# Row additions of a mixture-of-experts phase: two DMAs of 512 columns against four of 256, and loads that wait for a landing

## The chip, the cores and the metric

One core of a Trainium2 chip runs the whole program. The metric is the device time of one execution in microseconds (us), lower is better. The kernel before takes 1786.95 us, the median of 3 runs (1781.33 to 1793.82).

## What is computed

The input has 16 x 256 = 4096 rows of 512 floats. Four residual layers follow each other: a cross-attention over latents, a LoRA layer with gates, an attention with 8 heads, and a mixture of 64 experts. The change lies in the last one:

```
probs = softmax(xf @ router_weight)              # xf: normalised rows, 4096 x 512
topw, topi = top_k(probs, 8); topw /= sum(topw)
xe = zeros(64, 256, 512); xe[expert, slot] = xf[token]     # up to CAP = 256 slots an expert
h  = silu(xe @ gate_proj) * (xe @ up_proj)       # 512 -> 192
ye = h @ down_proj                               # 192 -> 512
out[token] += ye[expert, slot] * weight          # a token is in up to 8 experts
```

All is float32.

## The kernel before

**Two phases.** The first, to about 1190 us, runs the attention layers for 16 batches. It writes each batch's result to `out_rows` in DRAM, and GpSimd scatters the normalised rows to `slot_rows` in DRAM (L1484), each with its row number in column 512 and its 64 expert weights behind that. The second phase, the expert phase, takes the 64 experts one after the other. An expert has 256 slots, worked on as two halves of 128: unit `u = 2 * expert + half`.

**Loads of an expert, on SyncE's queue.** `load_rows(e)` (L537) brings 577 KB of slots into one of NB = 5 buffers `x_slots`; `load_weights(e)` brings 768 KB of gate and up weights (L525) and 384 KB of down weights (L529). After a first batch of loads, SyncE's loop waits until the additions of expert e have been issued (the semaphore `adds_issued`, L552), and then issues the rows of expert e + 5 and the weights of expert e + 7.

**Work of a unit.** TensorE turns the slots (L791), multiplies by gate and up in three products of split floats (L802 to L804), turns the hidden values (L813) and multiplies by down (L825 to L829). ScalarE and VectorE split values and weights into a high and a low part and apply silu. ScalarE's L1038 scales the result by the expert weight and writes it into `y_slots`, a ring of NY = 3 buffers of an expert each. Before it writes a buffer again it waits for the landing of the additions that read it (L1037). VectorE's `copy_ids` (L1324) copies the 256 row numbers into `row_ids`, one of NI = 6 buffers.

**Row additions, on GpSimd.** `add_rows(u)` issues one indirect DMA (L1526) that adds 128 rows of 512 floats from `y_slots` to the rows of `out_rows` named by `row_ids`. Two experts may hold the same token, so the additions of expert e wait until both DMAs of expert e - 1 have landed (L1523, L1524). The two DMAs of one expert are issued one behind the other. After the second a small memset of `issue_mark` (L1531) raises `adds_issued`.

GpSimd has nothing else to do in the expert phase, and its additions stand in the order of the experts. SyncE's queue holds only the loads in the order of the experts. The kernel ends when the last additions have landed (L559).

Of the kernel before, what the change touches and what calls it, by code (L numbers as in the profile page):

```python
# [7 lines left out]
ALU = mybir.AluOpType  # L8
# [5 lines left out]
I32 = mybir.dt.int32  # L14
U32 = mybir.dt.uint32

P = 128
# [122 lines left out]
def build(nc, a, out, slots_dram, dims):  # L140
    B, HALF, T, L, NHEAD, DQ, NE, NEXP, CAP, TOPK, NRANK = (
        dims[k] for k in ("B", "HALF", "T", "L", "NHEAD", "DQ", "NE", "NEXP", "CAP", "TOPK", "NRANK"))
# [3 lines left out]
    ROWS = B * HALF * P  # L146
# [10 lines left out]
    NX = 4  # L157
    NB = 5
    NW = 3
    NY = 3  # L160
    NI = 6
    ND = 3
    BC = NHEAD * C
# [23 lines left out]
    with stack:  # L187
        def sem(name):
            return stack.enter_context(nc.semaphore(name))

        def sb(name, shape, dt=F32, on=stack):
            return on.enter_context(nc.sbuf_tensor(name, shape, dt))
# [5 lines left out]
        free = [sem(f"bank_free{i}") for i in range(8)]  # L198
# [14 lines left out]
        fill_ready = sem("fill_row_ready")  # L213
# [49 lines left out]
        weights_of = [sem(f"expert_weights_in{i}") for i in range(NB)]  # L263
        down_of = [[sem(f"down_pair_in{i}_{k}") for k in range(2)] for i in range(ND)]
        rows_of = [sem(f"expert_rows_in{i}") for i in range(NB)]
        adds_issued = sem("adds_issued")
        added = [[sem(f"added{i}_{q}") for q in range(2)] for i in range(2)]
        xt_hi_ok = sem("xt_hi_ok")
        gu_hi_ok = sem("gu_hi_ok")
        gu_lo_ok = sem("gu_lo_ok")  # L270
# [2 lines left out]
        row_ids_ok = sem("row_ids_ok")  # L273
# [18 lines left out]
        row_no = A("row_no", [P, 2])  # L292
# [15 lines left out]
        fill_row = rows[1]  # L308
# [80 lines left out]
        issue_mark = sb("issue_mark", [P, 1])  # L389
        row_ids = [sb(f"row_ids{i}", [P, 2, 1], I32) for i in range(NI)]  # L390


# [4 lines left out]
        U = 2 * NEXP  # L397

        full_a = [BC * B // 2] * 4 + [0] + taken
# [14 lines left out]
        def _(e):  # L414
# [134 lines left out]
            for e_ in range(NEXP):  # L549


                w.wait_ge(adds_issued, e_ + 1)  # L552
                if e_ + NB < NEXP:
                    load_rows(e_ + NB)
                if e_ + NB + 2 < NEXP:
                    load_weights(e_ + NB + 2)
            for i in range(2):
                for q in range(2):
                    w.wait_ge(added[i][q], 16 * (NEXP // 2))  # L559
            w.wait_ge(slots_filled, 16 * (NEXP + 1))  # L560

        @block.tensor
# [280 lines left out]
        def _(e):  # L843
# [189 lines left out]
            def down(u):  # L1033
                e_, s = divmod(u, 2)
                w.wait_ge(full[6 + u % 2], full_a[6 + u % 2] + u // 2 + 1)
                if e_ >= NY:
                    w.wait_ge(added[(e_ - NY) % 2][s], 16 * ((e_ - NY) // 2 + 1))  # L1037
                e.activation(ye[e_ % NY][:, s, :], psum[6 + u % 2][:, :], ACT.Copy,  # L1038
                             scale=xe[e_ % NB][:, s, T + 1 + e_:T + 2 + e_]).then_inc(free[6 + u % 2], 1)

# [22 lines left out]
        def _(e):  # L1063
# [162 lines left out]
            def dispatch(b, what, _):  # L1226
# [7 lines left out]
                elif what in ("rows0", "rows1"):  # L1234
# [8 lines left out]
                    e.tensor_scalar(rw[:, k, T:T + 1].bitcast(I32), row_no[:, 0:1], float((b * HALF + k) * P), None,  # L1243
                                    ALU.add)
                elif what == "peak":
                    bank, _ = filled("disp", "route", b)
# [71 lines left out]
            def copy_ids(e_):  # L1318
                i = e_ % NB
                w.wait_ge(rows_of[i], 16 * (e_ // NB + 1))  # L1320
                if e_ >= NI:
                    w.wait_ge(added[(e_ - NI) % 2][0], 16 * ((e_ - NI) // 2 + 1))
                    w.wait_ge(added[(e_ - NI) % 2][1], 16 * ((e_ - NI) // 2 + 1))
# [73 lines left out]
        def _(e):  # L1397
# [105 lines left out]
            e.memset(fill_row[:, :, :], 0.0).then_inc(pool_step, 1)  # L1503
            w.wait_ge(pool_step, step.up())
            for c in range(2):
                e.iota(fill_row[:, c, T:T + 1].bitcast(I32), pattern=[[0, 1]], base=ROWS + c * P,
                       channel_multiplier=1).then_inc(fill_ready, 1)
            e.iota(row_no[:, :], pattern=[[P, 2]], base=0, channel_multiplier=1,
                   allow_small_or_imprecise_dtypes=True).then_inc(pool_ready, 1)
            for _, ev in gpsimd_order:  # L1510
                if ev[0] == "prep":
# [70 lines left out]
```

## Time and profile before

| | |
|---|---|
| median of 3 runs | 1786.95 us |
| runs | 1781.33, 1786.95, 1793.82 us |
| profiled execution | 1788.09 us, span 1785.9 us |
| mean granted TensorE clock | 0.944 |

The span is the time from the first to the last instruction of the profiled execution. A busy share is the share of a stretch in which an engine executed something; for the DMA it is the time that the packets took, as a share of 16 engines' time. The share can go somewhat over 100% in a short stretch, since a packet is counted where it starts and neighbouring packets overlap a little. In the chain of work that ended last, "issue" is time in which an engine waited for nothing that the profile shows.

### The profile page before, as it was taken

The page shows a single profiled execution, that of the slowest core. Times are in us where ns is not written, and L with a number is a line of the kernel's source. Part 1 is how long each engine was busy: PE and PEld are TensorE (multiplying, and loading weights), DVE is VectorE, ACT ScalarE, POOL GpSimd, SP SyncE. Part 2 cuts the span into 40 slices and gives each one's busy share as a digit, 9 for nine tenths or more (in the row PEclk, how much of TensorE's full clock was granted, in tenths as well). Part 3 has the DMA queues.
Part 4 walks back from the last instruction along what each step waited for, and adds up shares of the span by engine and source line. Part 5 has one row for each costly group of instructions (what it writes and reads, how often), then busy time and mean ns, then how long its engine had stood idle before and what let it go on. Part 6 is the DMA issues. An engine that isn't in the chain of part 4 may idle for free.

```text
span 1785.9 us, 25234 instructions
## 1 busy us (share of the span) xinstructions
PE 1572.3 (88%) x8016; PEld 1004.1 (56%) x8016; DVE 1253.0 (70%) x2994; ACT 973.9 (55%) x1938; POOL 796.8 (45%) x889
## 2 busy tenths in 40 slices
PE   5899999989999999999999889616999999999994
PEld 2444455444454454454444444215999887888883
DVE  2477778767768767777777677235888777787782
ACT  3455675655665665665655644313666555565562
POOL 4122326444464564563554445653444333334343
PEclk8889999999999999999999999857999999999997
DMA  9957654453463363352333222026999999999995
GB/s 329 299 168 248 225 143 127 141 180 109 129 211 105 120 197 92 105 156 86 94 92 94 79 59 64 25 82 231 268 289 256 267 259 259 263 263 266 274 250 81
DMA packets 150387, 311.91 MB, mean 175 GB/s; under 512 B 27674, under 2 KB 37786, under 8 KB 150256
## 3 DMA queue, kind: packets, MB, share of 16 engines
q1 hardware_dynamic: 111344, 238.89, 40.0%
q0 software_dynamic: 38912, 71.43, 20.1%
q8 instruction: 64, 1.05, 0.2%
q14 instruction: 67, 0.55, 0.1%
HBM read 141.25 MB, written 155.91 MB: 166 GB/s over the span
## 4 chain that ended last, share of the span: by engine, by line
PE 51%; DMA 14%; DVE 10%; issue 7%; POOL 5%; another core or an unknown queue 4%; SPq 4%; ACT 3%; DVEq 1%; POOLq 0%; ACTq 0%
DMA out_rows<-y_slots,row_ids 12%; PE bank L693 7%; PE bank L705 5%; PE bank L684 5%; POOL out_rows L1526 4%; PE bank L662 3%; PE bank L727 3%; PE bank L607 2%; DVE max_col L1202 2%; PE bank L613 2%; PE bank L802 2%; SPq L489 2%; PE bank L804 2%; PE bank L803 2%
## 5 line engine op out<-in xcount | busy, mean ns | idle before, releaser
L1202 DVE TENSOR_REDUCE max_col<-bank 128x1 f32<-128x512 f32 x512 | 340.7, 683 | 169.2 <-PE bank L684 145.9
L966 ACT ACTIVATE p_t<-bank 128x512 f32<-128x512 f32 x512 | 294.4, 596 | 212.5 <-PE bank L693 189.3
L1526 POOL DMA_INDIRECT out_rows<-y_slots,row_ids x128 | 212.7, 1662 | 344.9 <-DMA out_rows<-y_slots,row_ids 250.2
L1484 POOL DMA_INDIRECT slot_rows<-row,slot_i x256 | 255.2, 997 | 77.5 <-issue 76.6
L693 PE MATMUL bank<-q_stack,k_stack 98*128 98x512 f32 x512 | 277.8, 545 | 6.0 <-ACT p_t L966 4.1
L1472 POOL TENSOR_TENSOR p_sum<-p_t 128x512 f32<-128x512 f32 x128 | 168.4, 1322 | 206.5 <-ACT p_t L966 203.2
L684 PE MATMUL bank<-k_stack,q_stack 96*128 96x512 f32 x512 | 214.0, 419 | 4.6 <-DVE max_col L1202 4.2
L693 PEld LDWEIGHTS bank<-q_stack,k_stack 98*128 98x128 f32 x512 | 98.1, 193 | 192.6 <-issue 166.4
L802 PE MATMUL bank<-gate_up_hi,x_slots_t_hi 128*128 128x384 f32 x512 | 184.4, 360 | 2.8 <-DVE x_slots_t_lo L1330 2.6
L804 PE MATMUL bank<-gate_up_hi,x_slots_t_lo 128*128 128x384 f32 x512 | 173.0, 338 | 0.0
L803 PE MATMUL bank<-gate_up_lo,x_slots_t_hi 128*128 128x384 f32 x512 | 172.9, 338 | 0.0
L1038 ACT ACTIVATE y_slots<-bank,x_slots 128x512 f32<-128x512 f32 x128 | 88.2, 689 | 100.8 <-PE bank L829 97.3
L705 PE MATMUL bank<-p_t,v_t 128*32 128x512 f32 x1024 | 138.4, 613 | 0.2 <-DVE head_sb L1218 0.2
L662 PE MATMUL bank<-base_w,x_t 128*128 128x512 f32 x256 | 132.7, 633 | 0.0
L791 PE MATMUL bank<-ident,x_slots 128*128 128x128 f32 x512 | 79.6, 279 | 60.0 <-DMA x_slots<-slot_rows 59.9
L684 PEld LDWEIGHTS bank<-k_stack,q_stack 96*128 96x128 f32 x512 | 99.6, 195 | 53.1 <-issue 29.3
L1355 DVE TENSOR_TENSOR gate_up_lo<-gate_up,gate_up_hi 128x768 fp32r<-128x768 f32 x128 | 121.7, 951 | 0.0
L1330 DVE TENSOR_TENSOR x_slots_t_lo<-bank,x_slots_t_hi 128x512 fp32r<-128x512 f32 x128 | 87.5, 683 | 35.5 <-ACT x_slots_t_hi L1018 35.0
L1048 ACT CAST gate_up_hi<-gate_up 128x768 fp32r<-128x768 f32 x128 | 105.5, 825 | 10.7 <-DMA gate_up<-in_gate_up 10.7
L791 PEld LDWEIGHTS bank<-ident,x_slots 128*128 128x128 f32 x512 | 62.2, 142 | 85.5 <-issue 38.5
L1024 ACT ACTIVATE silu<-bank 128x192 f32<-128x192 f32 x128 | 42.5, 332 | 111.1 <-PE bank L804 109.2
L1401 POOL TENSOR_SCALAR row_rstd<-row_mv 128x2 f32<-128x2 f32 x48 | 11.0, 229 | 205.0 <-DVE row_mv L1088 205.0
(186 smaller groups left out, 3298.3 us busy)
## 6 DMA issues: line engine op xcount, KB each, us to landing
gate_up<-in_gate_up SPq DMA_DIRECT2D x64, 768.0 KB
slot_rows<-row SPq DMA_DIRECT2D x64, 577.0 KB, 7.9
x_slots<-slot_rows SPq DMA_DIRECT2D x64, 577.0 KB, 5.5
k_stack<-prob SPq DMA_DIRECT2D x192, 128.0 KB, 3.8
down<-in_down SPq DMA_DIRECT2D x64, 384.0 KB
q_stack<-x_t SPq DMA_DIRECT2D x128, 128.0 KB
x<-in_x SPq DMA_DIRECT2D x16, 512.0 KB, 3.3
ctx<-in_ctx SPq DMA_DIRECT2D x16, 512.0 KB, 4.3
```

What stands on the lines that cost most here:

```text
L662: e.matmul(bank[:, :], x_t[:, k, c, :], base_w[:, c, :], start=c == 0, stop=False)
L684: e.matmul(psum[2 + n % 2][:, :], q_st[b % 2][0:SK, head, c * P:(c + 1) * P], k_st[b % 2][0:SK, head, :], start=True, stop=True).then_inc( ...
L693: e.matmul(psum[n % 2][:, :], k_st[b % 2][0:SKM, head, j * P:(j + 1) * P], q_st[b % 2][0:SKM, head, :], start=True, stop=True).then_inc(fu ...
L705: m = e.matmul(psum[4][h * DQ:(h + 1) * DQ, :], v_t[b % 2][:, j, head + h, :], p_t[step % 2][:, h, :], start=j == 0, stop=j == C - 1)
L802: e.matmul(bk[:, 0:2 * INNER], xt_hi[u % 3][:, c, :], gu_hi[nw][:, c, :], start=c == 0, stop=False)
L803: e.matmul(bk[:, 0:2 * INNER], xt_hi[u % 3][:, c, :], gu_lo[nw][:, c, :], start=False, stop=False)
L804: m = e.matmul(bk[:, 0:2 * INNER], xt_lo[u % 3][:, c, :], gu_hi[nw][:, c, :], start=False, stop=c == C - 1)
L966: e.activation(p_t[step % 2][:, h, :], psum[n % 2][:, :], ACT.Exp, scale=SCALE).then_inc(free[n % 2], 1)
L1202: e.tensor_reduce(max_col[quad % 2][:, h, c:c + 1], psum[2 + n % 2][:, :], X, ALU.max, negate=True).then_inc(free[2 + n % 2], 1)
L1472: e.tensor_tensor(p_sum[:, h, :], p_t[(step - 1) % 2][:, h, :], p_t[step % 2][:, h, :], ALU.add).then_inc(p_sum_ok, 1)
L1484: e.indirect_dma_start(out=slots_dram, in_=rows[b % 2][:, k, :], in_offset=None, out_offset=bass.IndirectOffsetOnAxis(ap=slot_i[b % 2][:, ...
L1526: e.indirect_dma_start(out=out, out_offset=bass.IndirectOffsetOnAxis(ap=row_ids[e_ % NI][:, q, :].bitcast(U32), axis=0), in_=ye[e_ % NY][: ...
```

## The change

The two DMAs of an expert become four: the left 256 columns of both halves of the slots, then the right 256 columns of both. `out_rows` is viewed as twice as many rows of 256 floats; the row numbers are doubled where they are made, and the right part uses an element offset of 256. The left parts of expert e wait for the landing of the left parts of expert e - 1 alone, the right parts for the right parts. `adds_issued` and the memset are gone: SyncE waits for the landing of the left parts of expert e before it issues the rows of expert e + 5 and the weights of expert e + 7. `y_slots` gets a fourth buffer. The waits of ScalarE, VectorE and the end of the kernel name the semaphores of both parts.

```diff
-    NY = 3
+    NY = 4
-        adds_issued = sem("adds_issued")
-        added = [[sem(f"added{i}_{q}") for q in range(2)] for i in range(2)]
+        added = [[[sem(f"added{i}_{part}_{q}") for q in range(2)] for part in range(2)] for i in range(2)]
@@ SyncE, loop over the experts
-                w.wait_ge(adds_issued, e_ + 1)
+                w.wait_ge(added[e_ % 2][0][0], 16 * (e_ // 2 + 1))
+                w.wait_ge(added[e_ % 2][0][1], 16 * (e_ // 2 + 1))
                 if e_ + NB < NEXP:
                     load_rows(e_ + NB)
                 if e_ + NB + 2 < NEXP:
                     load_weights(e_ + NB + 2)
@@ ScalarE, down
                 if e_ >= NY:
-                    w.wait_ge(added[(e_ - NY) % 2][s], 16 * ((e_ - NY) // 2 + 1))
+                    w.wait_ge(added[(e_ - NY) % 2][0][s], 16 * ((e_ - NY) // 2 + 1))
+                    w.wait_ge(added[(e_ - NY) % 2][1][s], 16 * ((e_ - NY) // 2 + 1))
@@ GpSimd
-            def add_rows(u):
-                e_, q = divmod(u, 2)
-                if q == 0:
-                    w.wait_ge(row_ids_ok, e_ + 1)
-                    if e_:
-                        w.wait_ge(added[(e_ - 1) % 2][0], 16 * ((e_ - 1) // 2 + 1))
-                        w.wait_ge(added[(e_ - 1) % 2][1], 16 * ((e_ - 1) // 2 + 1))
-                w.wait_ge(free[6 + q], full_a[6 + q] + e_ + 1)
-                e.indirect_dma_start(
-                    out=out, out_offset=bass.IndirectOffsetOnAxis(ap=row_ids[e_ % NI][:, q, :].bitcast(U32), axis=0),
-                    in_=ye[e_ % NY][:, q, :], in_offset=None, compute_op=ALU.add).then_inc(added[e_ % 2][q], 16)
-                if q == 1:
-                    w.wait_ge(adds_issued, e_)
-                    e.memset(issue_mark[:, :], 0.0).then_inc(adds_issued, 1)
-
-            for u in range(U):
-                add_rows(u)
+            half_rows = out.rearrange("r (k t) -> (r k) t", k=2)
+
+            def add_rows(e_, part):
+                w.wait_ge(row_ids_ok, e_ + 1)
+                if e_:
+                    w.wait_ge(added[(e_ - 1) % 2][part][0], 16 * ((e_ - 1) // 2 + 1))
+                    w.wait_ge(added[(e_ - 1) % 2][part][1], 16 * ((e_ - 1) // 2 + 1))
+                for q in range(2):
+                    w.wait_ge(free[6 + q], full_a[6 + q] + e_ + 1)
+                    e.indirect_dma_start(
+                        out=half_rows, in_=ye[e_ % NY][:, q, part * T // 2:(part + 1) * T // 2], in_offset=None,
+                        out_offset=bass.IndirectOffsetOnAxis(ap=row_ids[e_ % NI][:, q, :].bitcast(U32), axis=0),
+                        element_offset=part * T // 2, compute_op=ALU.add).then_inc(added[e_ % 2][part][q], 16)
+
+            for e_ in range(NEXP):
+                for part in range(2):
+                    add_rows(e_, part)
```

The rest of the diff doubles the row numbers (two iotas, one added constant) and names the new semaphores in the waits of VectorE's `copy_ids` and of the end.

## Rows read from the trace of the kernel before

**Rows 1.** The page: engine totals, and the span in 40 slices.
```profile
PE 1572.3 (88%) x8016; PEld 1004.1 (56%) x8016; DVE 1253.0 (70%) x2994; ACT 973.9 (55%) x1938; POOL 796.8 (45%) x889
DMA  9957654453463363352333222026999999999995
```

**Rows 2.** Busy time by stretch: early experts, late experts, last three additions alone.
```profile
core 0: us, PE busy (x) PEld busy (x) DVE busy (x) ACT busy (x) POOL busy (x), PEclk, DMA share, GB/s
1373.00:1755.00 382.00, 358.09 (x2043) 320.33 (x2042) 298.81 (x661) 220.74 (x443) 150.77 (x133) 1.00 0.95 257
1246.00:1364.00 118.00, 118.00 (x695) 108.82 (x694) 104.91 (x230) 74.91 (x151) 49.46 (x42) 1.00 0.99 274
1757.00:1779.00 22.00, 3.93 (x18) 2.58 (x16) 1.25 (x4) 2.75 (x6) 8.71 (x9) 0.66 0.53 71
```

**Rows 3.** The additions, whole phase: duration ns min/median/max, first and last start; landing.
```profile
L1526 POOL DMA_INDIRECT out_rows<-y_slots,row_ids x128: 1544/1555/2289, 1236.7 to 1779.9; - x128
...
DMA to landing us min/median/max: 4.6/5.5/7.2
```

**Rows 4.** The chain that ended last, 1505 to 1535 us, two periods of it.
```profile
1514.64 1.56 POOL out_rows L1526
1516.20 0.30 issue
1516.51 5.01 DMA out_rows<-y_slots,row_ids
...
1521.65 0.71 issue
1522.36 1.56 POOL out_rows L1526
1523.92 0.30 issue
1524.22 5.44 DMA out_rows<-y_slots,row_ids
```

**Rows 5.** DMA queues, 1400 to 1700 us: q1 the loads, q0 the additions.
```profile
DMA packets 29256, 79.62 MB, mean 265 GB/s; under 512 B 2763, under 2 KB 2763, under 8 KB 29230
...
q1 hardware_dynamic: 19301, 61.21, 52.5%
q0 software_dynamic: 9929, 18.09, 44.6%
q8 instruction: 13, 0.21, 0.3%
q14 instruction: 13, 0.11, 0.1%
```

**Rows 6.** DMA queue of the additions without loads, 1757 to 1779 us.
```profile
q0 software_dynamic: 854, 1.55, 53.1%
```

**Rows 7.** The same queue: 1765.8 to 1766.2 us, later in it.
```profile
DMA packets 37, 0.07 MB, mean 184 GB/s; under 512 B 1, under 2 KB 1, under 8 KB 37
...
q0 software_dynamic: 37, 0.07, 100.5%
```

**Rows 8.** The same queue: 1764.6 to 1765.0 us, the start of that DMA.
```profile
q0 software_dynamic: 20, 0.04, 124.9%
```

**Rows 9.** The additions' queue, 1768.84 to 1769.0 us: completion writes only.
```profile
q0 software_dynamic: 4, 0.00, 3.8%
```

**Rows 10.** DMA queues, 571.0 to 571.6 us: loads in packets of 1024 B.
```profile
q1 hardware_dynamic: 199, 0.20, 94.6%
```

**Rows 11.** DMA queue, 945.8 to 946.4 us: loads in packets of 2048 B.
```profile
q1 hardware_dynamic: 115, 0.23, 98.8%
```

**Rows 12.** GpSimd from 1495 us: one expert's two additions and the memset.
```profile
1498.27 1.60 POOL L1526 DMA_INDIRECT out_rows<-y_slots,row_ids  x1 [6.82 <-issue]
1500.18 1.54 POOL L1526 DMA_INDIRECT out_rows<-y_slots,row_ids  x1 [0.31 <-issue]
1501.17 0.67 POOL L1531 MEMSET issue_mark<- 128x1 f32 x1
```

**Rows 13.** SyncE's queue from 1495 us: the loads issued behind those additions.
```profile
1501.87 0.38 SPq L537 DMA_DIRECT2D x_slots<-slot_rows  x1
1502.29 0.47 SPq L525 DMA_DIRECT2D gate_up<-in_gate_up  x1
1502.80 0.48 SPq L529 DMA_DIRECT2D down<-in_down  x1
```

**Rows 14.** Waits, 1400 to 1700 us: us in total, times, longest.
```profile
POOL out_rows L1526 <- DMA out_rows<-y_slots,row_ids: 129.8, 27, 6.4
POOL out_rows L1526 <- ACT y_slots L1038: 32.8, 6, 6.0
PEld bank L791 <- DMA x_slots<-slot_rows: 31.6, 28, 2.8
PE bank L791 <- DMA x_slots<-slot_rows: 20.0, 21, 2.3
```

**Rows 15.** Who waited for the additions' landing, whole phase.
```profile
  ACT y_slots L1038: 1.9, 2
```

More of the change, by code:

```diff
@@ L388, in build @@
         ye = [sb(f"y_slots{i}", [P, 2, T]) for i in range(NY)]
-        issue_mark = sb("issue_mark", [P, 1])
         row_ids = [sb(f"row_ids{i}", [P, 2, 1], I32) for i in range(NI)]
@@ L557, in _ @@
             for i in range(2):
-                for q in range(2):
-                    w.wait_ge(added[i][q], 16 * (NEXP // 2))
+                for part in range(2):
+                    for q in range(2):
+                        w.wait_ge(added[i][part][q], 16 * (NEXP // 2))
             w.wait_ge(slots_filled, 16 * (NEXP + 1))
@@ L1242, in dispatch @@
                                     ALU.mult).then_inc(rows_ok, 1)
-                    e.tensor_scalar(rw[:, k, T:T + 1].bitcast(I32), row_no[:, 0:1], float((b * HALF + k) * P), None,
+                    e.tensor_scalar(rw[:, k, T:T + 1].bitcast(I32), row_no[:, 0:1], float(2 * (b * HALF + k) * P), None,
                                     ALU.add)
@@ L1321, in copy_ids @@
                 if e_ >= NI:
-                    w.wait_ge(added[(e_ - NI) % 2][0], 16 * ((e_ - NI) // 2 + 1))
-                    w.wait_ge(added[(e_ - NI) % 2][1], 16 * ((e_ - NI) // 2 + 1))
+                    for part in range(2):
+                        for q in range(2):
+                            w.wait_ge(added[(e_ - NI) % 2][part][q], 16 * ((e_ - NI) // 2 + 1))
                 e.tensor_copy(row_ids[e_ % NI][:, :, :], xe[i][:, :, T:T + 1].bitcast(I32)).then_inc(row_ids_ok, 1)
@@ L1505, in _ @@
             for c in range(2):
-                e.iota(fill_row[:, c, T:T + 1].bitcast(I32), pattern=[[0, 1]], base=ROWS + c * P,
-                       channel_multiplier=1).then_inc(fill_ready, 1)
-            e.iota(row_no[:, :], pattern=[[P, 2]], base=0, channel_multiplier=1,
+                e.iota(fill_row[:, c, T:T + 1].bitcast(I32), pattern=[[0, 1]], base=2 * (ROWS + c * P),
+                       channel_multiplier=2).then_inc(fill_ready, 1)
+            e.iota(row_no[:, :], pattern=[[2 * P, 2]], base=0, channel_multiplier=2,
                    allow_small_or_imprecise_dtypes=True).then_inc(pool_ready, 1)
@@ L1516, in _ @@
                     dispatch(*ev[1:])
-            def add_rows(u):
-                e_, q = divmod(u, 2)
-                if q == 0:
-                    w.wait_ge(row_ids_ok, e_ + 1)
-                    if e_:
-                        w.wait_ge(added[(e_ - 1) % 2][0], 16 * ((e_ - 1) // 2 + 1))
-                        w.wait_ge(added[(e_ - 1) % 2][1], 16 * ((e_ - 1) // 2 + 1))
-                w.wait_ge(free[6 + q], full_a[6 + q] + e_ + 1)
-                e.indirect_dma_start(
-                    out=out, out_offset=bass.IndirectOffsetOnAxis(ap=row_ids[e_ % NI][:, q, :].bitcast(U32), axis=0),
-                    in_=ye[e_ % NY][:, q, :], in_offset=None, compute_op=ALU.add).then_inc(added[e_ % 2][q], 16)
-                if q == 1:
-                    w.wait_ge(adds_issued, e_)
-                    e.memset(issue_mark[:, :], 0.0).then_inc(adds_issued, 1)
-            for u in range(U):
-                add_rows(u)
+            half_rows = out.rearrange("r (k t) -> (r k) t", k=2)
[4 more added lines that the diff above has]
+                    w.wait_ge(added[(e_ - 1) % 2][part][1], 16 * ((e_ - 1) // 2 + 1))
+                for q in range(2):
+                    w.wait_ge(free[6 + q], full_a[6 + q] + e_ + 1)
[4 more added lines that the diff above has]
+            for e_ in range(NEXP):
+                for part in range(2):
+                    add_rows(e_, part)
 def kernel(x, ctx_2048, L0_xattn_theta_w, L0_xattn_theta_b, L0_xattn_phi_w, L0_xattn_phi_b, L0_xattn_g_w,
```

## The prediction

> **What bounds the kernel now.** I read the page first. TensorE is busiest over the whole span, but the slices show two regimes: from about 1190 us on the DMA engines stand at 9 tenths or more, where they had 2 to 6 before [rows 1]. The change touches only that stretch, the expert phase. Next I cut it in stretches [rows 2]. From 1246 to 1364 us TensorE has no gap at all: 695 matmuls in 118 us. From 1373 to 1755 us it is busy 358 of 382 us. A unit needs 3 x 4 matmuls for gate and up, 4 + 2 transposes and 5 for down, 23 in all, so an expert has 46, and the first stretch gives 118 x 46 / 695 = 7.81 us an expert: TensorE's own pace.
>
> The additions are slower. Their first issue is at 1236.7 us, and the last of 128 at 1779.9 us [rows 3]. With 1.86 us from an expert's first to its second (below) that is 63 periods in 541.3 us, 8.6 us each. So TensorE starts ahead, the ring of row buffers runs out, and from then on the additions set the pace. The chain of waits shows how a period is built [rows 4]: 1.56 us to issue the first DMA, 0.30 us, then 5.01 us from the issue of the second to its landing, and 0.83 us until the next expert's issue, 7.7 us in all. The same links with a landing of 7.2 us [rows 3] give 9.9 us. What lies between 7.7 and 9.9 is the DMA's state.
>
> That state is the real bound, and this is where the reader should count. From 1400 to 1700 us 2763 packets are under 512 B; these are the completion writes, 16 for each DMA, so 80 for an expert with 3 loads and 2 additions. That is 34.5 experts, 8.70 us each [rows 5]. The check: 9929 packets of additions are 288 an expert, 256 rows and 32 completions. The loads take 52.5% x 8.70 = 4.57 us of every DMA engine, the additions 44.6% x 8.70 = 3.88 us, the rest 0.03. Sum 8.48 of 8.70 us: 97.5% full. The additions' share is not a product of crowding: with no load beside them 854 packets, 2.97 experts, take 53.1% of 22 us, 3.93 us an expert [rows 6]. Speeding up the chain alone cannot win much; the DMA engines' time has to fall.
>
> **The change part by part.** *Packets.* An expert's additions become 4 DMAs of 128 rows of 1 KB: 512 row packets and 64 completions. An engine has 8 row packets in each DMA, as before, so before it had 16 and now it has 32. What does one cost? In the later part of an undisturbed DMA 36 row packets (one more is a completion) take 100.5% of 16 x 0.4 us: 178 ns each for 2 KB [rows 7]. At its start 20 packets take 124.9% of the same 6.4 us: 400 ns each [rows 8]. So a DMA has a start-up on each engine. Its size follows from the sum: 3.88 us less 2 completions of 0.024 us [rows 9] is 3.83, or 1.92 us a DMA; less 8 x 0.178 = 1.42 that is 0.49 us of start-up.
>
> No row shows an addition of 1 KB. For plain loads 199 packets of 1 KB take 94.6% of 9.6 us, 45.6 ns [rows 10], and 115 packets of 2 KB take 98.8%, 82.5 ns [rows 11]: half the bytes cost 0.55 of the time. Applied to 178 ns that is 98 ns. For the start-up the ends are half of it (it goes with the bytes) and all of it (it is the latency of a first access). The first packet alone has 400 - 178 = 222 ns of it, which I keep whole because a wait for a first answer does not shrink with the bytes; of the other 0.27 I take three quarters: 0.42 us. Then an expert's additions cost 4 x (8 x 0.098 + 0.42) + 0.10 = 4.92 us in place of 3.88.
>
> The bounds: with everything by bytes it is 3.93 (only the completions are added), and with the whole start-up and the packet at 0.66 of 178 ns, 4 x (0.94 + 0.49) + 0.10 = 5.82. If a packet cost the same at any size it would be 7.7. I take 4.92 as nearest to the rows of the start and of the packet sizes.
>
> The Trainium skill bears on this and speaks for less. "DMA: Bandwidth & Descriptors", section "Why small descriptors are slow (HBM only)", gives an overhead of about 3 cycles a packet beside 32 bytes a cycle: 35 cycles for 1 KB and 67 for 2 KB. By that the additions would cost 3.88 x 70 / 67 = 4.05 us as an estimate from the page. The trace agrees roughly for the plain packets (0.55 of the time) and not for the start of an addition, which the rule does not have.
>
> *The period after.* 4.57 + 4.92 + 0.03 = 9.52 us of each engine, and at the same fullness, 9.52 / 0.975 = 9.77 us an expert, 1.07 us more.
>
> *GpSimd.* An issue takes 1.56 us and the next can follow 0.30 us later [rows 4, 12]. Four of them are 7.4 us an expert where two were 3.7, and if each part's first pays the 0.71 us after a wait [rows 4] it is 8.3 us. The memset of 0.67 us goes; it lay in the wait for the landing [rows 12] and gives nothing. GpSimd stays under 9.77, hidden behind the DMA. If that cover were gone it would be the bound at 7.4 to 8.3, near TensorE's 7.81.
>
> *The chain of waits.* It is split in two that overlap: 1.86 us, the landing, 0.83 us for each part, while the other part is issued inside the landing. Landings under 6.2 us, most of today's, would leave it at or below 8.9, so it does not bind either. Its gain is real and cannot be cashed in.
>
> *Loads later.* Today the rows' load is issued 3.60 us after an expert's first addition (1501.87 against 1498.27) [rows 12, 13]. After the change it is 1.86 + 4.6 to 5.5 + about 0.2, 6.7 to 7.6 us [rows 3], so 3 to 4 us later. Behind this wait stand the rows of expert e + 5 and the weights of e + 7, and TensorE's transposes wait for the rows. They do so today for 28 times and at most 2.8 us [rows 14], not because the load is slow but because it is issued at the additions' pace; the additions in turn mostly wait for their own landing, 129.8 us, and for `y_slots` 32.8 us in 6 waits. So finished results stand ready before them, and a load that comes 3 to 4 us later eats from that stock once and not in every period. Over 5 experts of 9.77 us the slack grows by 5.3 us, more than it eats. Price nothing; if the stock were empty, up to 4 us for every fifth expert, 0.8 us a period, and that stands within the upper end.
>
> *The fourth buffer.* ScalarE waited 1.9 us in all for the three [rows 15]. Nothing to gain. The other waits (VectorE's ids, six buffers) lie further back.
>
> **Sum.** Of the 63 periods the last three have no loads beside them and stay near 7.7 us, 60 grow: 60 x 1.07 = 64 us. The span goes from 1785.9 to 1850 us, the profiled execution from 1788.1 to 1852. It stands 1 us above the median, so I give 1851 us for the median of the runs.
>
> **The rivals.**
> *By bytes.* The start-up goes with the bytes, or loads fill it, and an expert's additions cost 3.9 to 4.1 us. Then the period is 8.49 to 8.7 / 0.975 = 8.7 to 8.9 us, the time 1787 to 1800. For it: the page's rule named above would give 8.65 / 0.975 = 8.87 us and 1797; the packet of 1 KB costs 0.55. Against it: 400 ns at the start of a DMA that had no neighbour [rows 8].
>
> *The chain was the bound (the other sign).* The time that packets take at a start is latency in which an engine can serve the other queue; with parts in turn the queues mix well and this time stops counting. The additions then cost 32 x 0.098 + 0.10 = 3.2 us, the sum 7.8 / 0.975 = 8.0, and the period is the larger of that and GpSimd's 7.4 to 8.3, some 8.15: 60 x 0.55 = 33 us less, 1754. It decides as soon as the additions' engine time falls under 3.6 us, since a period of (4.57 + 3.6 + 0.03) / 0.975 = 8.4 us takes 60 x 0.3 = 18 us off, 1%. For it: the chain that ended last runs through the additions and their landings. Against it: their share is the same with and without loads beside them [rows 5, 6], and the engines are full at 97.5%.
>
> *By packets.* A packet costs nearly the same at any size: 2 x 3.88 = 7.8 us, 12.7 us a period, 1787 + 60 x 4.0 = 2027. The loads' two sizes speak against it [rows 10, 11].
>
> **How the numbers follow.** My forecast (period 9.2 to 10.6, 1815 to 1900) gets 0.62, by bytes 0.16, the chain 0.17, by packets 0.05. The predicted time is 1851. A measurement of this kernel can tell about 1%, 18 us. By packets and my forecast are slower, and a little of the by-bytes case too: 0.68. The rest of that case is within 1%: 0.14. The chain case is faster, with a little from beside it: 0.18. The range leaves out the chain case's centre and the packet case: 1765 to 1895, about 0.8. My forecast's own range is 1820 to 1890.
>
> **What the profile after would show.** The additions' queue at about 50% share with 576 packets an expert, 4.9 us of engine time in a stretch without loads too; if it shows 4.0, the by-bytes case is right. The period of the additions 9.8 us. The loads' engine time still 4.57 us an expert. GpSimd busy 6.2 to 6.6 us an expert with gaps. TensorE's waits for `x_slots` grow to about 2 us an expert, 9.77 less 7.81. I am wrong if the start-up does not repeat in each DMA, if the engines were less full than 97.5% in truth, or if a load issued late leaves the engines idle, which would show as a DMA share well below 0.95 together with longer waits for `x_slots`.

## The result and the profile after

| | before | after |
|---|---|---|
| median of 4 runs | 1784.14 us | 1859.59 us |
| runs | 1768.06 to 1793.82 | 1841.09 to 1865.20 |
| profiled execution, span | 1785.9 us | 1839.3 us |

The ratio is 1.041, 95% interval 1.030 to 1.052: slower, by 75 us on the medians. The forecast was 1851 us. The number came out close, but by luck: the rest of this document shows that none of its three terms (the additions' price, the loads' price, the fullness of the DMA engines) did.

The profiled spans differ by 53 us only: the profiled execution of the kernel after is the fastest of its four runs, and it entered the expert phase early. The additions' own lines are the better measure: their first and last start stand in one line.

```profile
L1529 POOL DMA_INDIRECT out_rows<-y_slots,row_ids x256: 1539/1544/2624, 1200.8 to 1833.4; - x128
```

Against [rows 3] the expert phase lasts 632.6 us in place of 543.2, but it begins 36 us earlier, at 1200.8 in place of 1236.7. The first phase does the same work in both kernels; it varied from one profiled execution to another (later ones began the additions at 1145 to 1156 us). So below I read periods of the additions and not spans.

The DMA queues from 1400 to 1700 us, to be held against [rows 5]:

```profile
DMA packets 33783, 68.09 MB, mean 227 GB/s; under 512 B 3330, under 2 KB 18580, under 8 KB 33760
...
q1 hardware_dynamic: 16605, 52.19, 50.8%
q0 software_dynamic: 17155, 15.62, 34.4%
```

An expert now has 512 + 64 = 576 packets of additions and 560 of loads (512 + 48). So 17155 / 576 = 29.8 experts in 300 us, a period of 10.07 us. The additions take 34.4% x 10.07 = 3.47 us of an engine (before 3.88). The loads are 16605 / 560 = 29.65 experts and take 50.8% x 300 / 29.65 = 5.14 us (before 4.57). The sum is 8.6 us, hardly more than before, yet the period is 1.4 us longer: the engines are 86% full where they were 97.5%.

Busy time, the same stretch and then two microseconds at a time over one period. The second last column is the DMA share. These are to be held against [rows 2].

```profile
core 0: us, PE busy (x) PEld busy (x) DVE busy (x) ACT busy (x) POOL busy (x), PEclk, DMA share, GB/s
1400.00:1700.00 300.00, 250.54 (x1372) 221.60 (x1370) 205.12 (x450) 150.77 (x299) 195.42 (x119) 0.97 0.86 227
...
1503.00:1505.00 2.00, 2.00 (x12) 1.70 (x12) 1.38 (x4) 0.59 (x2) 0.93 (x1) 1.00 0.75 116
1505.00:1507.00 2.00, 2.00 (x15) 2.00 (x14) 1.97 (x6) 1.90 (x3) 1.70 (x2) 1.00 0.45 99
1507.00:1509.00 2.00, 2.00 (x13) 1.71 (x12) 1.99 (x6) 0.59 (x2) 1.69 (x2) 1.00 1.03 394
1509.00:1511.00 2.00, 2.00 (x15) 2.00 (x13) 1.96 (x5) 1.90 (x3) 1.70 (x2) 1.00 1.07 318
1511.00:1513.00 2.00, 2.00 (x13) 1.70 (x13) 2.00 (x7) 0.67 (x3) 0.75 (x1) 1.00 1.16 264
1513.00:1515.00 2.00, 2.00 (x14) 2.00 (x13) 1.96 (x3) 1.82 (x3) 1.07 (x1) 1.00 0.54 80
```

There is a hole between 1504 and 1506, and the next begins at 1514, one period later. What stands at its edges? First GpSimd, then SyncE's queue:

```profile
1504.07 1.72 POOL L1529 DMA_INDIRECT out_rows<-y_slots,row_ids  x1 [2.78 <-DMA out_rows<-y_slots,row_ids]
1506.10 1.96 POOL L1529 DMA_INDIRECT out_rows<-y_slots,row_ids  x1 [0.30 <-issue]
1508.36 1.54 POOL L1529 DMA_INDIRECT out_rows<-y_slots,row_ids  x1 [0.31 <-issue]
1510.21 1.54 POOL L1529 DMA_INDIRECT out_rows<-y_slots,row_ids  x1 [0.30 <-issue]
1513.93 1.94 POOL L1529 DMA_INDIRECT out_rows<-y_slots,row_ids  x1 [2.18 <-DMA out_rows<-y_slots,row_ids]
```

```profile
1504.85 0.38 SPq L535 DMA_DIRECT2D x_slots<-slot_rows  x1
1505.27 0.47 SPq L523 DMA_DIRECT2D gate_up<-in_gate_up  x1
1505.78 0.43 SPq L527 DMA_DIRECT2D down<-in_down  x1
1514.64 0.38 SPq L535 DMA_DIRECT2D x_slots<-slot_rows  x1
```

And the chain that ended last, in the same place, against [rows 4]:

```profile
1506.10 7.08 DMA out_rows<-y_slots,row_ids
1513.18 0.02 issue
...
1513.93 0.70 POOL out_rows L1529
1514.63 0.04 issue
...
1516.18 6.93 DMA out_rows<-y_slots,row_ids
```

Counted from the first of the 256 additions, 1504.07 and 1506.10 are the right pair of one expert, 1508.36 and 1510.21 the left pair of the next. So four additions go out in one run, and then GpSimd waits. The right pair of the expert before has landed at 1503.3, which releases 1504.07. The left pair that went out at 1497.90 and 1499.75 has its last packets at 1504.4, and its landing releases the loads at 1504.85, 0.8 us behind the first addition of the run and 1.2 us ahead of its second. The loads' first packets come at 1505.8. The run's first addition packets come only at 1508.8, near 5 us after its issue: from 1506.0 to 1508.5 the engines served 301 packets of loads and none of an addition. The right pair lands at 1513.2, 7.1 us after its second issue, where a pair took 5.0 to 5.4 before. The run's last packets are through at 1514.2, and from there to 1515.6 no packet runs.

This landing sets the period. The chain that ended last, from 1400 to 1700 us, by its parts:

```profile
by line: DMA out_rows<-y_slots,row_ids 76.0%; issue 18.8%; POOL out_rows L1529 8.2%; POOLq L29 0.6%
```

The parts sum to somewhat over 100%, since pieces that reach over an edge of the window count whole. The chain has 31 landings, one in each period, of 6.5 to 9.0 us with a median of 7.4, and 1.86 + 7.4 + 0.83 = 10.1 us is the period. GpSimd waits for a landing once in each expert:

```profile
POOL out_rows L1529 <- DMA out_rows<-y_slots,row_ids: 76.0, 29, 4.5
```

TensorE waits for rows 47.4 us by its weight loads where it waited 31.6 [rows 14]:

```profile
PEld bank L791 <- DMA x_slots<-slot_rows: 47.4, 27, 4.1
```

### The profile page after: what moved, and what is told of

Its sections match the earlier page's. It is cut to its first block, busy times and chain, and to the rows that moved or that the text cites. A ratio compares the mean times of both kernels' runs of the same rounds, so it can differ in the third digit from the quotient of the medians.

```text
span 1839.3 us, 25478 instructions
## 1 busy us (share of the span) xinstructions
PE 1579.0 (86%) x8016; PEld 1007.2 (55%) x8016; DVE 1257.2 (68%) x2994; ACT 974.6 (53%) x1938; POOL 992.2 (54%) x953
## 4 chain that ended last, share of the span: by engine, by line
PE 41%; DMA 24%; issue 10%; DVE 9%; POOL 6%; another core or an unknown queue 3%; SPq 3%; ACT 3%; DVEq 1%; POOLq 0%; ACTq 0%
DMA out_rows<-y_slots,row_ids 23%; PE bank L693 7%; PE bank L705 5%; PE bank L684 5%; POOL out_rows L1529 4%; PE bank L727 3%; PE bank L662 3%; PE bank L607 2%; DVE max_col L1203 2%; SPq L487 2%; PE bank L620 2%; PE bank L613 2%; PE bank L635 2%; DVE x L1225 1%
## 5 line engine op out<-in xcount | busy, mean ns | idle before, releaser
L1529 POOL DMA_INDIRECT out_rows<-y_slots,row_ids x256 | 416.9, 1629 | 237.6 <-DMA out_rows<-y_slots,row_ids 154.2
L1203 DVE TENSOR_REDUCE max_col<-bank 128x1 f32<-128x512 f32 x512 | 339.7, 682 | 141.8 <-PE bank L684 134.5
L802 PE MATMUL bank<-gate_up_hi,x_slots_t_hi 128*128 128x384 f32 x512 | 191.4, 374 | 19.5 <-DVE x_slots_t_lo L1332 18.8
L803 PE MATMUL bank<-gate_up_lo,x_slots_t_hi 128*128 128x384 f32 x512 | 178.7, 349 | 0.0
L804 PE MATMUL bank<-gate_up_hi,x_slots_t_lo 128*128 128x384 f32 x512 | 178.6, 349 | 0.0
L791 PE MATMUL bank<-ident,x_slots 128*128 128x128 f32 x512 | 83.5, 288 | 108.4 <-DMA x_slots<-slot_rows 108.2
L1370 DVE CAST down_mixed<-down 64x512 fp32r<-64x512 f32 x64 | 27.3, 426 | 162.8 <-issue 153.1
L662 PE MATMUL bank<-base_w,x_t 128*128 128x512 f32 x256 | 126.8, 608 | 0.0
L802 PEld LDWEIGHTS bank<-gate_up_hi,x_slots_t_hi 128*128 128x128 f32 x512 | 102.2, 200 | 24.7 <-DVE x_slots_t_lo L1332 23.6
```

Source lines behind the costliest of these rows:

```text
L662: e.matmul(bank[:, :], x_t[:, k, c, :], base_w[:, c, :], start=c == 0, stop=False)
L802: e.matmul(bk[:, 0:2 * INNER], xt_hi[u % 3][:, c, :], gu_hi[nw][:, c, :], start=c == 0, stop=False)
L803: e.matmul(bk[:, 0:2 * INNER], xt_hi[u % 3][:, c, :], gu_lo[nw][:, c, :], start=False, stop=False)
L804: m = e.matmul(bk[:, 0:2 * INNER], xt_lo[u % 3][:, c, :], gu_hi[nw][:, c, :], start=False, stop=c == C - 1)
L1203: e.tensor_reduce(max_col[quad % 2][:, h, c:c + 1], psum[2 + n % 2][:, :], X, ALU.max, negate=True).then_inc(free[2 + n % 2], 1)
L1529: e.indirect_dma_start(out=half_rows, in_=ye[e_ % NY][:, q, part * T // 2:(part + 1) * T // 2], in_offset=None, out_offset=bass.IndirectOf ...
```

## The experiments

They ran on three chips, each measured against the kernel before on the same chip (medians 1727.6, 1719.5 and 1727.0 us). Ratios compare with that. "Period" and engine times are worked out as above from the DMA queues between 1330 and 1630 us. At the end of the section a table holds all of them.

### Halves, loads released by an issue

The kernel after with one thing put back.

```diff
-                w.wait_ge(added[e_ % 2][0][0], 16 * (e_ // 2 + 1))
-                w.wait_ge(added[e_ % 2][0][1], 16 * (e_ // 2 + 1))
+                w.wait_ge(adds_issued, e_ + 1)
...
                 for part in range(2):
                     add_rows(e_, part)
+                    if part == 0:
+                        w.wait_ge(adds_issued, e_)
+                        e.memset(issue_mark[:, :], 0.0).then_inc(adds_issued, 1)
```

> The kernel after (four DMAs of 256 columns, four buffers) with one thing put back: the loads wait for the issue of the left pair's additions, by a mark from GpSimd, and no longer for their landing. Theory gate (the late load costs all): from 1400 to 1700 us the additions of the kernel after take 34.4% and the loads 50.8% of the DMA time, 86% in all, and the engines stand nearly idle between the landing of the left parts and the first packet of the loads issued behind it. With the loads issued earlier that hole closes; the additions take 3.5 us and the loads 4.6 to 5.1 us of an expert, so the period is 8.3 to 8.9 us, the 63 periods last 525 to 560 us (before 541, after 627), and the time is within 1.5% of the kernel before, 1765 to 1800 us. Theory packets (what the prediction said: packets of 1 KB and their start-up cost the engines 1 us an expert): the period stays near 9.8 us and the time near 1850.

Measured: 1744.20 us, ratio 1.009 (1.006 to 1.013).

```profile
q1 hardware_dynamic: 18210, 57.81, 56.5%
q0 software_dynamic: 18443, 16.80, 41.5%
```

The engines are full again, 98%. The period is 9.37 us. The additions cost 3.89 us, the loads 5.21. As a ratio the time lies in the band of the gate theory, within 1.5% of the kernel before. The period lies above its 8.3 to 8.9, since the sum of both is 9.1 us and not 8.1 to 8.6. The theory from the prediction (1850 us, 9.8 us) is out: most of the loss is not the packets.

### Whole rows, loads released by the landing

The other part of the change alone, on the kernel before.

```diff
-                w.wait_ge(adds_issued, e_ + 1)
+                w.wait_ge(added[e_ % 2][0], 16 * (e_ // 2 + 1))
+                w.wait_ge(added[e_ % 2][1], 16 * (e_ // 2 + 1))
```

> The kernel before (two DMAs of 512 columns, three buffers) with one thing changed: the loads wait for the landing of both additions of the expert and not for their issue. Theory gate: the loads of one expert and the additions of the next start together and then leave the engines idle together; additions 3.9 us and loads 4.6 us plus a hole of 1.5 to 2 us give a period of 10 to 10.5 us, the time 1865 to 1900. Theory packets: the wait alone costs nothing that shows, 1787 us, at most 1% more.

Measured: 1804.65 us, ratio 1.046 (1.044 to 1.048). The period is 10.34 us. One period, two microseconds at a time:

```profile
1504.00:1506.00 2.00, 1.24 (x6) 0.67 (x4) 2.00 (x6) 1.21 (x4) 1.70 (x3) 1.00 0.97 334
1506.00:1508.00 2.00, 0.86 (x7) 0.86 (x8) 1.56 (x3) 0.85 (x2) 0.49 (x2) 1.00 1.03 307
1508.00:1510.00 2.00, 2.00 (x14) 1.97 (x13) 0.69 (x1) 0.48 (x2) 0.00 (x0) 1.00 1.08 292
1510.00:1512.00 2.00, 2.00 (x14) 1.73 (x13) 1.69 (x5) 1.21 (x4) 0.00 (x0) 1.00 0.65 124
1512.00:1514.00 2.00, 2.00 (x14) 1.97 (x13) 1.96 (x4) 1.35 (x4) 0.48 (x1) 1.00 0.12 22
```

The hole is here too: 12% in the two microseconds around the landing at 1512.7, since that one event releases loads and additions alike, the loads 0.8 us ahead of the expert's first addition. From 1503 to 1507 us only loads have packets (73 to 102% of the engines), and those of the additions come behind. The expectation of 10 to 10.5 us held. The expected times, 1865 to 1900 us, had been written for the first chip, where they are ratios of 1.045 to 1.065, so the ratio stands at the lower end of them. So the wait costs this much with no half row anywhere. Not all of it need come by the landing: from 1330 to 1630 us GpSimd's wait ended with a landing 18 times and 11 times with the row numbers, which VectorE copies out of the loaded rows.

```profile
POOL out_rows L1527 <- DMA out_rows<-y_slots,row_ids: 119.0, 18, 7.8
POOL out_rows L1527 <- DVE row_ids L1325: 72.6, 11, 7.1
```

How much the row numbers add beyond the landing was not measured.

### No wait on additions at all

Both kernels with the release taken out; a load waits for its buffer alone.

> The kernel after without any wait on the additions before a load: a load waits for its buffer alone. Theory gate: no hole, so the DMA engines are full again, and the period is the sum of additions and loads, 8.6 to 9.2 us, 1780 to 1825. The danger is that loads now stand in the queue all the time and each landing of additions becomes longer, 7 us and more; then the chain of a part, 1.86 + 7 + 0.83 us, makes 9.7 us, and the time stays near 1850. Theory packets: 9.8 us a period and 1850 as well.

> The kernel before without any wait on the additions before a load. Theory gate: what paces the loads there does not cost, the engines are 97.5% full already, so the period stays at 8.6 to 8.8 us if landings do not grow; as the loads then always compete with the additions, landings of 6.5 to 7.5 us in place of 5.5 are likely, which makes 1.86 + 7 + 0.83 = 9.7 us and 1850. Theory packets says nothing else than the sum: 8.7 us, 1787.

Measured: halves 1799.35 us, 1.042 (1.040 to 1.044), period 10.67 us, share 84%. Whole rows 1846.48 us, 1.069 (1.066 to 1.072), period 11.17 us, share 75%. My first number for each (full engines, 8.6 to 9.2) was wrong and the danger named behind it was what happened, and by more than I had worked out (9.7 us a period), for whole rows above all. The waits show it: from 1400 to 1700 us ScalarE now waits for the landing before it may write a result, 134.5 us with whole rows,

```profile
ACT y_slots L1037 <- DMA out_rows<-y_slots,row_ids: 134.5, 34, 8.6
```

where it waited 1.9 us in the whole kernel before [rows 15]. The mark that paces the loads is worth 7% to the kernel before.

### Earlier and later marks

Whole rows. The mark stands behind the first addition (`w_early`), or its memset writes 1152 or 2304 columns and so ends 1 or 2 us later.

```diff
-                if q == 1:
+                if q == 0:
                     w.wait_ge(adds_issued, e_)
```

```diff
-        issue_mark = sb("issue_mark", [P, 1])
+        issue_mark = sb("issue_mark", [P, 1152])
```

> The kernel before with the mark behind the expert's first addition and not its second: the loads are issued about 1.9 us earlier. Theory phase: loads now come before the additions are through, both share the engines, landings grow from 5.5 to 6.5 us or more, period 9.2 to 10 us, 2 to 5% slower. Theory late (earlier is better or the same): at most 8.7 us and the same time.

> The kernel before with a longer mark: the memset behind the second addition writes 1152 columns and not 1, so the loads are issued about 1 us later, 4.6 us behind the expert's first addition in place of 3.6. Theory phase (what the loads' wait sets is when loads and additions meet at the engines; additions that find loads queued ahead lose the start-up cost, 182 ns a packet of 2 KB in the kernel whose loads wait for the landing against 240 ns before): additions 3.2 to 3.5 us an expert in place of 3.9, no hole yet, period 8.0 to 8.5 us, 0.5 to 2.5% faster. Theory late (any later load opens a hole and costs in proportion, 1.7 us a period for 3.3 us of delay): 1 us later costs 0.3 to 0.5 us a period, 1.0 to 1.7% slower.

> The kernel before with a mark of 2304 columns, which issues the loads about 5.7 us behind the expert's first addition, 2 us later than before. With 1 us (1152 columns) the time was the same, 0.999: the additions' share fell from 45.9 to 42.0% and the loads' rose from 45.9 to 51.0%. Theory phase: 2 us later more of the additions' start falls beside loads, the sum of both stays, period 8.8 to 9.1 us, within 1%. Theory hole: the last additions of the expert are through at about 6 us and the first packet comes at 7.7, so the engines stand idle 1 to 1.5 us: period 9.3 to 9.8, 1.5 to 3% slower.

Measured: early 1895.62 us, 1.104 (1.098 to 1.109), period 11.90 us, share 70%; 1 us later 1717.70 us, 0.999 (0.997 to 1.001), 8.82 us; 2 us later 1732.28 us, 1.003 (1.000 to 1.006), 9.21 us. The same stretch of the unchanged kernel before had 9.09 us. The first trace of it had 8.79 us there, so differences of 0.3 us between periods of two traces say nothing. "Earlier is better or the same" is out by far, and the cost of an early release was more than twice what I expected. A release 1 to 2 us later by an issue costs nothing that shows (0.999 and 1.003), so lateness by itself is not what hurts in the kernel after. Both of my numbers for 1152 columns were wrong, the gain of 0.5 to 2.5% and the loss of 1.0 to 1.7%. With 2304 columns the time is within 1%, as the phase theory said, and the period 0.1 us above its range; the hole theory (1.5 to 3% slower) is out. Where the gain of 1152 columns went can be read:

```profile
q1 hardware_dynamic: 19061, 60.25, 56.7%
q0 software_dynamic: 9792, 17.83, 40.8%
```

The additions fell from 4.07 to 3.60 us an expert and the loads rose from 4.60 to 5.00: the work that no longer waits in one queue waits in the other.

The early release shows what goes wrong. First GpSimd, then SyncE's queue, then the engines in four stretches:

```profile
1510.79 1.84 POOL L1526 DMA_INDIRECT out_rows<-y_slots,row_ids  x1 [7.77 <-issue]
...
1512.93 2.12 POOL L1526 DMA_INDIRECT out_rows<-y_slots,row_ids  x1 [0.19 <-issue]
```

```profile
1512.77 0.38 SPq L537 DMA_DIRECT2D x_slots<-slot_rows  x1
```

```profile
1512.50:1514.50 2.00, 0.42 (x2) 0.00 (x0) 1.12 (x2) 0.00 (x0) 1.81 (x3) 1.00 0.70 73
1514.50:1518.00 3.50, 0.00 (x0) 0.00 (x0) 0.00 (x0) 1.41 (x2) 0.55 (x1) 0.69 1.05 344
1518.00:1521.50 3.50, 3.39 (x12) 3.39 (x13) 0.00 (x0) 0.59 (x1) 0.00 (x0) 0.50 0.94 272
1521.50:1524.50 3.00, 3.00 (x15) 2.69 (x15) 2.21 (x8) 0.72 (x3) 1.67 (x2) 0.80 0.01 3
```

The loads go out 0.2 us ahead of the second addition. The first addition's packets run from 1513.0 to 1515.6. From 1515.6 to 1518 there are 285 packets of loads and none of an addition, and the second addition gets its first packet at 1518.4, 5.5 us after its issue. Both are through at 1521.5, and then the engines stand at 1% for 3 us, until the next pair. No landing released these loads.

### Halves, released by the fourth issue

```diff
-                    if part == 0:
+                    if part == 1:
```

> The kernel after with the loads waiting for the issue of the expert's fourth addition, not for the landing of the left parts. That is about 7.5 us behind its first addition, nearly when the left parts land, 7 to 8 us, but without a wait on a landing. Theory gate by time: it is the moment of the load that costs, so this runs like the kernel after, period 9.8 to 10.3 us, 4% slower than before. Theory gate by landing (a late landing delays loads, which delay the next landing): this is clearly better than the kernel after, period below 9.6.

Measured: 1744.18 us, 1.016 (1.011 to 1.020), period 9.38 us, 96% full. The loads go out 7.3 to 8.4 us behind the expert's first addition, median 7.6, where the kernel after has 6.1 to 8.7, median 6.9, and it runs like the variant with the mark behind the second issue. "Gate by time" is out. But two things differ from the kernel after: the release does not hang on a landing, and the loads now go out 1.7 us behind the last addition of a run of four and not behind its first.

### Halves, released by another landing

```diff
-                w.wait_ge(added[e_ % 2][0][0], 16 * (e_ // 2 + 1))
-                w.wait_ge(added[e_ % 2][0][1], 16 * (e_ // 2 + 1))
+                if e_:
+                    w.wait_ge(added[(e_ - 1) % 2][1][0], 16 * ((e_ - 1) // 2 + 1))
+                    w.wait_ge(added[(e_ - 1) % 2][1][1], 16 * ((e_ - 1) // 2 + 1))
```

> The kernel after with the loads waiting for the landing of the right parts of the expert before, which comes about 1.5 to 2 us earlier in the period than that of the left parts of this expert. Theory hole: the loads' first packets come about 2 us behind their release, and in the kernel after no addition is queued in that time; released earlier, they come when left parts are still under way, so the hole shrinks by as much: DMA share 0.90 to 0.94, period 9.3 to 9.7 us. Theory landing (any release by a landing runs in a loop with the additions and costs the same): 10.0 us or more.

Measured: 1796.26 us, 1.039 (1.032 to 1.046), period 10.23 us, share 85%, as in the kernel after (1.038, 10.22 us, 85%). The loads now go out 0.4 to 1.6 us behind the expert's first addition. My theory that the hole shrinks with this place is out. But the place is hardly another one. The four additions of an expert now go out as one run, and the loads, at 1504.27, again fall between the first and the second of it:

```profile
1503.70 1.76 POOL L1530 DMA_INDIRECT out_rows<-y_slots,row_ids  x1 [3.97 <-DMA out_rows<-y_slots,row_ids]
1505.76 1.54 POOL L1530 DMA_INDIRECT out_rows<-y_slots,row_ids  x1 [0.30 <-issue]
```

In the kernel after the run begins with the right pair of an expert, here with the left one; the loads have the same place in it. So this run does not show that any landing does it.

### The fourth buffer, and the unchanged kernels again

> The kernel after with three result buffers in place of four. The additions trail the results by less than three experts and ScalarE waited for a buffer nowhere in the kernel after; so no change, within 1% of the kernel after, period 10 to 10.3 us. Were the fourth buffer doing work, this would be slower by 1% or more with waits of ScalarE for landings.

> The kernel after, unchanged, on the chip of the other experiments if it is the same one. Its period should again be 10 to 10.3 us with the DMA engines 85% full, its time 4% over the kernel before; beside it the variant whose loads wait for the issue (1.009 of before) shows what the wait for the landing costs, 3%.

> The kernel before, unchanged, for its trace beside the others of this chip. The periods of the additions should again be 8.6 to 8.8 us with the DMA engines 97% full; the first phase may last otherwise than in the first trace (there the first addition came at 1236.7 us, in the kernel after at 1200.8, on the second chip near 1152).

Measured: three buffers 1800.16 us, 1.041 (1.034 to 1.048); the kernel after again 1796.11 us, 1.038 (1.033 to 1.044); the kernel before again 1720.47 us, one run, with a period of 9.09 us and engines 95% full where I had expected 8.6 to 8.8 and 97%. The fourth buffer does nothing that shows. The two unchanged kernels, before and then after:

```profile
q1 hardware_dynamic: 18493, 58.46, 50.6%
q0 software_dynamic: 9504, 17.31, 44.8%
```

```profile
q1 hardware_dynamic: 16620, 52.72, 51.5%
q0 software_dynamic: 16907, 15.40, 33.7%
```

### All of them side by side

Engine time of one expert in us, 1330 to 1630 us of each trace. "Full" is the two queues' share. The third column is where the load of the rows goes out among the additions, by the medians of the same stretch; a "run of four" is four additions that GpSimd issues 1.85 us apart before it waits.

| kernel | release of the loads | loads go out | ratio | period | additions | loads | full |
|---|---|---|---|---|---|---|---|
| before | 2nd issue | 1.7 behind the pair's 2nd | 1 | 9.09 | 4.07 | 4.60 | 95% |
| whole, 1152 columns | 2nd issue + 1 us | 2.7 behind the pair's 2nd | 0.999 | 8.82 | 3.60 | 5.00 | 98% |
| whole, 2304 columns | 2nd issue + 2 us | 3.6 behind the pair's 2nd | 1.003 | 9.21 | 3.68 | 5.12 | 95% |
| whole, early | 1st issue | 0.2 ahead of the pair's 2nd | 1.104 | 11.90 | 3.49 | 4.86 | 70% |
| whole, none | buffers alone | ahead of the pair's 2nd (19 of 27) or its 1st (8) | 1.069 | 11.17 | 2.97 | 5.36 | 75% |
| whole, landing | both landed | 0.8 ahead of the pair's 1st | 1.046 | 10.34 | 2.96 | 5.45 | 80% |
| halves, issue | 2nd issue | 1.7 behind the left pair's 2nd | 1.009 | 9.37 | 3.89 | 5.21 | 98% |
| halves, 4th issue | 4th issue | 1.7 behind the 4th | 1.016 | 9.38 | 3.88 | 5.14 | 96% |
| halves, none | buffers alone | ahead of the run's 2nd (25 of 29) | 1.042 | 10.67 | 3.63 | 5.29 | 84% |
| after | left landed | 1.2 ahead of the run's 2nd | 1.038 | 10.22 | 3.44 | 5.21 | 85% |
| after, 3 buffers | left landed | 1.2 ahead of the run's 2nd | 1.041 | 10.10 | 3.45 | 5.17 | 85% |
| halves, other landing | right of e - 1 landed | 1.2 ahead of the run's 2nd | 1.039 | 10.23 | 3.47 | 5.18 | 85% |

The two engine times together lie between 8.3 and 9.1 us in every row. What differs is how full the engines are. In the five rows at 95 to 98% the loads go out behind a pair of additions. In the seven at 70 to 85% they go out ahead of a pair or between its two additions, whether a landing, an issue or nothing at all released them.

## Why the prediction came out

**The bound: right before the change, wrong after it.** Before, the engines are 97.5% full. After, they are 86% full and the chain of waits is the bound, of which the prediction said: "Landings under 6.2 us, most of today's, would leave it at or below 8.9, so it does not bind either." The landings on the chain have a median of 7.4 us, and by the prediction's own sum that is 1.86 + 7.4 + 0.83 = 10.1 us, the measured period. Splitting the chain in two brought nothing: GpSimd still waits for one landing in each expert, and that landing had become longer. A period is still the engines' time divided by how full they are, but that is bookkeeping and holds for any bound. TensorE, GpSimd's own work and the fourth buffer do not decide. GpSimd is busy 195.42 / 29.8 = 6.6 us an expert, as forecast (6.2 to 6.6).

**The price of the additions: wrong where it counted.** The step "4 x (8 x 0.098 + 0.42) + 0.10 = 4.92 us in place of 3.88" is mis-sized for additions beside loads: 3.47 us. It is nearly right, 0.3 us too high, for what its rows showed, additions alone. Of the kernel after, 1806 to 1828 us, with no loads:

```profile
q0 software_dynamic: 1720, 1.57, 62.8%
```

1720 / 576 = 2.99 experts in 22 us at 62.8% are 4.63 us each. The start-up repeats in each DMA when nothing stands beside it. It goes when loads are queued at the same engines: whole rows cost 3.93 us alone [rows 6] and 2.96 beside loads (the landing variant), near 16 x 0.178 + 0.05 = 2.90, the packets with no start-up at all. In the kernel before the price was the same with and without loads, and I took that for a proof that loads do not matter. In its trace the two hardly overlap: from 1505.5 to 1508.5 us the loads have 101.7% and the additions one packet, from 1509 to 1512 the additions have 98.2% and the loads 0.8%. The mark keeps them apart. I read one state of the overlap as a property of the packet. In its own way the rival "the chain was the bound" had this part right (the start-up stops counting once the queues mix) and the rest wrong.

**The price of the loads: missed.** I kept 4.57 us. They took 5.14, and 4.9 to 5.5 in every variant that mixes the queues. The gain in the additions is mostly given back here.

**How full: the step that failed most.** "At the same fullness, 9.52 / 0.975" assumed what the change touches. The measured period is (3.47 + 5.14 + 0.04) / 0.86. With my sum of 9.52 and the measured 86% it would have been 11.1 us. A sum 0.9 us too high and a fullness 11 points too high cancelled to 9.77 against 10.07. That is luck, and so is the right sign: most of the 4% comes from the wait that the prediction priced at nothing.

**Loads later: wrong.** "Price nothing" rested on the stock of rows and results ahead, which was there. It asked who waits for the load and not what the load's packets do to the additions beside it. Released by a landing, the loads cost 3% of the 4% (halves: 1.009 by an issue, 1.038 by the landing). The rest, 0.9 to 1.6%, comes with the halves themselves. The prediction had named the sign to look for, a DMA share well below 0.95 together with longer waits for rows, and that is what the trace shows.

**Why this moment costs.** Shown by the runs: the moment by itself is not it, since releases by an issue at 3.5 and 7.3 to 8.4 us (halves) and at 3.6, 4.7 and 5.7 us (whole rows) keep the engines at 95 to 98%. That a landing releases the loads is not the whole of it either, since an issue at 1.8 us leaves them at 70% and no release at all at 75 to 84%. What fits all twelve rows of the table is the order. Behind a pair of additions the loads fill the time in which the pair lands and the next one is issued: before the change a pair lands at 1513.8, the next issue starts at 1514.64 [rows 4], the loads keep the engines at 94 to 112% from 1513 to 1517 us, and the next pair's first packets come at 1516.8, without a hole. Ahead of a pair, or between its two additions, the loads' packets come before those of the additions, since a load has its first packet 1.0 us after its issue (1504.85 to 1505.8) and an addition 2.1 to 2.2 us (1498.27 to 1500.4, 1510.79 to 1513.0). The additions are then the last to be through, their landing grows from 5 to 7 us or more, and when it comes nothing is left for the engines until the next issue has had its own 1 to 2 us. That this is the mechanism is argued from the traces.

**What stays open.** No run sets the order apart from the kind of release: one that waits for a landing and yet sends the loads behind the next pair, or halves with the mark behind the first issue. Why the early mark (1.104) is worse than no mark at all (1.069) was not tried either. Nor was a version found that beats the kernel before; the best is 0.999.

## What to carry to other kernels

A wait that paces transfers can be worth more than the transfers' size. Here the loads fill the engines while the additions land and are issued again, as long as they go out behind a pair of additions (95 to 98% full in five kernels); ahead of one, or in the middle of it, they delay its landing and leave a hole (70 to 85% in seven). When a period is a sum of engine times divided by a fullness, ask of each edit what it does to the fullness too, and where the hole would lie. When a forecast lays a chain of waits aside on a condition ("landings under 6.2 us"), ask whether the change keeps that condition. And a price that is the same with and without company proves nothing unless the two really ran together.

## What the runs showed of the hardware

The start of an indirect addition of 2 KB rows cost about 0.49 us of each engine in every DMA when the engines had nothing else (an estimate from 400 ns a packet at first and 178 ns later), and next to nothing when loads were queued beside it (2.96 us an expert against 3.93). With 1 KB rows: 1720 packets alone cost 4.63 us an expert, 16907 beside loads 3.44. The loads in turn took 0.3 to 0.9 us an expert more than the 4.57 of the first trace. The sum stayed between 8.3 and 9.1 us in all twelve kernels. A load's first packet came 1.0 us after its issue, an addition's 2.1 to 2.2 us, but 4.7 and 5.5 us where loads' packets were ahead of it. The Trainium skill, "DMA: Bandwidth & Descriptors", section "Issuing engines are not separate DMA queues", says that transfers started by different engines run on the same 16 DMA engines and interleave. The runs agree and add a number: with 4.57 us of loads and 3.88 us of additions an expert, when they interleave decides over 10% of this kernel's time.
